# Two stacked cross-attention layers on one core: operands loaded already transposed, scalings broadcast through DRAM, the residual kept transposed

## The reference, cut to what matters

```
# layer 0, twice (s = "a" on ctx, s = "v" on fside), x: (128, 64, 128), ctx and fside: (128, 64, 64)
q = LN(x) @ Wq + bq;  k = LN(c) @ Wk + bk;  v = LN(c) @ Wv + bv          # LN with gain and bias, over the last axis
out_s = softmax(q k^T * 128**-0.5) v @ Wo + bo
r = out_a + out_v + x
x1 = LN(r) @ fc_W + fc_b + r
# layer 1, on ctx
w = softmax((x1 Wq1 + bq1)(ctx Wk1 + bk1)^T * 128**-0.5)
out = x1 + (w (ctx Wv1 + bv1)) @ Wo1 + bo1
```

## Time and profile before

| | us |
|---|---|
| device time, median of 3 runs | 169.53 (167.81 to 170.84) |
| span of the profiled execution, first to last instruction | 167.2 |
| its own device time | not listed apart from the three runs |
| PE busy, weight loads busy | 155.5, 121.7 |
| DVE, ACT, POOL busy | 131.4, 124.2, 76.4 |
| moved by DMA | 15.93 MB, of which 15.14 MB on SP's queue |

### The profile page before, as it was taken

How to read it: one execution, slowest core, us unless ns; L and a number is a source line. 1 busy time by engine, 2 the same in 40 slices (tenths; PEclk the granted TensorE clock), 3 DMA queues, 4 the chain that set the end, 5 groups by cost and what they waited for, 6 DMA issues and landing times.

```text
span 167.2 us, 6323 instructions
## 1 busy us (share of the span) xinstructions
PE 155.5 (93%) x2442; PEld 121.7 (73%) x2442; DVE 131.4 (79%) x400; ACT 124.2 (74%) x384; POOL 76.4 (46%) x104
## 2 busy tenths in 40 slices
PE   6799998999999999799999999989999999999682
PEld 6769674896689687767786787667788887995350
DVE  1693499999899789999999996497688997596531
ACT  3431559869988979599879788977978789866930
POOL 2026269789676523714979624194532022110210
PEclk9965579999999999999999999999999999999955
DMA  5999999900001010101010011001010100101113
GB/s 139 299 380 380 378 379 378 364 33 0 2 4 67 0 67 0 68 2 67 4 63 4 0 67 65 6 0 67 0 67 20 47 6 4 67 0 65 63 67 125
DMA packets 9982, 15.93 MB, mean 95 GB/s; under 512 B 1249, under 2 KB 3682, under 8 KB 9954
## 3 DMA queue, kind: packets, MB, share of 16 engines
q1 hardware_dynamic: 9522, 15.14, 25.1%
q10 hardware_dynamic: 432, 0.40, 1.0%
HBM read 11.35 MB, written 4.19 MB: 93 GB/s over the span
## 4 chain that ended last, share of the span: by engine, by line
PE 73%; DVE 9%; ACT 7%; issue 4%; DMA 3%; POOL 2%; ACTq 1%; POOLq 0%
PE ps L1526 9%; PE ps L1465 8%; PE ps L1508 7%; PE ps L1576 5%; PE ps L1516 5%; PE ps L1496 4%; PE ps L1541 4%; PE ps L1534 4%; PE ps L1485 4%; PE ps L1456 4%; PE ps L1475 4%; PE ps L1449 4%; DMA cf_sb<-in_cf 3%; PE ps L1568 3%; ACT exp L632 3%
## 5 line engine op out<-in xcount | busy, mean ns | idle before, releaser
L384 POOL TENSOR_TENSOR prob<-exp,rsum 128x512 f32<-128x512 f32 x16 | 16.7, 1042 | 23.5 <-DVE rsum L1025 23.5
L390 POOL TENSOR_TENSOR prob<-exp,rsum 128x256 f32<-128x256 f32 x16 | 9.8, 613 | 29.0 <-DVE rsum L1085 29.0
L356 POOL TENSOR_TENSOR z_sb<-x_sb,x_rstd 128x512 f32<-128x512 f32 x15 | 15.4, 1040 | 15.9 <-ACT x_rstd L543 14.1
L632 ACT ACTIVATE exp<-ps,exp_bias 128x64 f32<-128x64 f32 x64 | 19.2, 315 | 3.5 <-DVE exp_bias L1080 3.4
L1061 DVE SCALAR_TENSOR_TENSOR x_sb<-ps,res_rstd,res_sb 128x128 f32<-128x128 f32 x64 | 19.2, 342 | 0.2 <-issue 0.2
L1465 PE MATMUL ps<-zT_sb,m 128*128 128x512 f32 x32 | 17.8, 645 | 0.0
L1526 PE MATMUL ps<-wd,resT_sb 128*128 128x130 f32 x128 | 17.6, 280 | 0.0
L1508 PE MATMUL ps<-w,mix_sb 128*128 128x128 f32 x128 | 17.5, 280 | 0.0
L378 POOL TENSOR_TENSOR cfn_sb<-cf_scaled,cf_shift 128x512 f32<-128x512 f32 x15 | 15.6, 1042 | 4.0 <-issue 2.9
L1526 PEld LDWEIGHTS ps<-wd,resT_sb 128*128 128x128 f32 x128 | 15.6, 191 | 2.0 <-ACT resT_sb L609 1.5
L371 POOL TENSOR_TENSOR cf_scaled<-cf_sb,cf_rstd 128x512 f32<-128x512 f32 x15 | 15.4, 1043 | 2.7 <-ACT cf_rstd L555 2.5
(11 more groups left out here) (141 smaller groups left out, 384.2 us busy)
## 6 DMA issues: line engine op xcount, KB each, us to landing
x_sb<-in_x SPq DMA_DIRECT2D x16, 256.0 KB, 6.8
out<-out_sb SPq DMA_DIRECT2D x16, 256.0 KB, 2.0
cf_sb<-in_cf SPq DMA_DIRECT2D x15, 256.0 KB, 7.1
ct_sb<-in_ct SPq DMA_DIRECT2D x16, 128.0 KB, 7.9
w_sb<-in_w SPq DMA_DIRECT2D x1, 448.0 KB, 5.6
cf_sb<-in_cf ACTq DMA_DIRECT2D x1, 256.0 KB, 4.9
wq_sb<-in_wq ACTq DMA_DIRECT2D x1, 128.0 KB, 2.8
wt_sb<-in_wt SPq DMA_DIRECT2D x1, 128.0 KB, 4.0
```

Source lines behind the costliest of these rows:

```text
L356: pool.tensor_tensor(z_sb[:, g % Z_SLOTS, :, :], x_sb[:, g, :, :], wide_x(g), ALU.mult).then_inc(z_pool, 1)
L384: pool.tensor_tensor(prob0[:, g % PROB0_SLOTS, :, :, :], exp0[:, g % EXP0_SLOTS, :, :, :], wide0(rsum0, g), ALU.mult).then_inc(prob0_pool, 1)
L632: last = nc.scalar.activation(exp1[:, g % EXP1_SLOTS, p, :], ps[:, bank + u, v * S:(v + 1) * S], ACT.Exp, bias=exp1_bias[:, g, p:p + 1], a ...
```

## The change

What it does, in the order of a group's steps:

- The host gives two more arrays: `xt`, x transposed (256 KB a group), and `kt`, the keys transposed (256 KB a group). Inputs no longer stay whole in SBUF but go through rings (`X_SLOTS` 4, `XT_SLOTS` 8, `CF_SLOTS` 9, `KT_SLOTS` 3, `CT_SLOTS` 6), so loads on SP wait for readers.
- Groups 0 to 3 are normalized as before (`z`, `zT`, `scale_cf`, `shift_cf`, `cfT`). For groups 4 to 15 the normalizing is done on the transposed arrays. There the scalings lie along the free axis, the same for every partition. So for each of the batches 3 to 8 the scalings and shifts (`rows`, 40 columns) are transposed on PE (`turn_rows`), copied by ACT (`copy_rowsT`), stored to DRAM by SP (`store_rows`, 40 rows of 512 bytes), and read back by three SP transfers that fill all 128 partitions with 4 KB each: `spread_x` (every partition reads the same 4 KB), `spread_k` and `spread_s` (partitions 0 to 63 read one 4 KB piece, 64 to 127 another). As the transfers are issued, both sides of `spread_x` count 128 along their outermost dimension; `spread_k` and `spread_s` count 128 partitions on the SBUF side, but their DRAM side is 2 pieces, each repeated 64 times, so its outermost dimension counts 2. POOL then multiplies and adds whole tiles: `scale_xt`, `scale_kt`, `shift_kt`. `scale_cf` stays, for the values.
- `out0` is one product with 512 columns in place of four with 128, and comes out transposed. `residual` adds xt and a bias column and is kept transposed, so `copy_resT` goes; `resN` transposes it back for `stats_res`, which now reads PSUM.
- `x1` is split: ACT scales the four blocks of `dense` (`gain`), DVE makes the key biases (`key_biases`), PE transposes (`x1T`), DVE adds bias and residual in one instruction over 128 x 512 (`x1`); `copy_x1T` goes.
- For groups 1, 4, 7, 10, 13 and 15 `softmax0` takes its exponentials from PSUM in eight blocks of 64 columns, with the negated maximum as bias, and `diff_scores0` goes.
- Some folding work moves (biases of layer 0's output), more PE products without a use at the start (18 in place of 8), and all five orders are new.

The core of the diff:

```diff
+TURNED = [0, 1, 2, 3]
+BATCHES = [[0], [1], [2, 3], [4, 5], [6, 7], [8, 9], [10, 11], [12, 13], [14, 15]]
+SPREAD_FROM = 3
+EXP_BY_BLOCKS = [1, 4, 7, 10, 13, 15]
...
+            def store_rows(b):
+                at = b - SPREAD_FROM
+                sp.wait_ge(rowsT_copied, at + 1)
+                sp.dma_start(rows_dram[at, :, :], rowsT[:, at % SPREAD_SLOTS, :]).then_inc(rows_stored[at % SPREAD_SLOTS], 16)
+
+            def spread_x(b):
...
+                sp.dma_start(x_spread[:, at % SPREAD_SLOTS, :, :].rearrange("p g t -> p (g t)"),
+                             rows_dram[at, 0:8, :].rearrange("r t -> (r t)").unsqueeze(0).broadcast_to([D, 8 * P])
+                             ).then_inc(x_spread_in[at % SPREAD_SLOTS], 16)
+
+            def spread_k(b):
+                at = b - SPREAD_FROM
+                sp.wait_ge(rows_stored[at % SPREAD_SLOTS], 16 * (at // SPREAD_SLOTS + 1))
+                if at >= SPREAD_SLOTS:
+                    sp.wait_ge(ks_done, BATCHES[b - SPREAD_SLOTS][-1] + 1 - len(TURNED))
+                sp.dma_start(k_spread[:, at % SPREAD_SLOTS, :, :].rearrange("p g t -> p (g t)"),
+                             rows_dram[at, 8:24, :].rearrange("(h r) t -> h (r t)", h=2).unsqueeze(1
+                             ).broadcast_to([2, C, 8 * P])).then_inc(k_spread_in[at % SPREAD_SLOTS], 16)
...
+            def scale_kt(g):
...
+                spread_in(pool, k_spread_in, g)
+                need(pool, cfT_shifted, at - KS_SLOTS + 1)
+                pool.tensor_tensor(blocks(ks_sb[:, g % KS_SLOTS, :]), kt_sb[:, at % KT_SLOTS, :, :, :, :],
+                                   blocks(k_spread[:, slot, half, :]), ALU.mult).then_inc(ks_done, 1)
+
+            def shift_kt(g):
...
+                pool.wait_ge(ks_done, at + 1)
+                spread_in(pool, s_spread_in, g)
...
-            def softmax0(g):
-                act.wait_ge(diff0_done, g + 1)
-                prob0_ready(act, g - EXP0_SLOTS)
-                nc.scalar.activation(exp0[:, g % EXP0_SLOTS, :, :, :], diff0[:, g % DIFF0_SLOTS, :, :, :], ACT.Exp
-                                     ).then_inc(exp0_done, 1)
+            def softmax0(g, bank):
+                need(act, prob0_done, g - EXP0_SLOTS + 1)
+                if g in EXP_BY_BLOCKS:
+                    act.wait_ge(max0_done, g + 1)
+                    for h in range(2):
+                        for p in range(PAIRS):
+                            last = nc.scalar.activation(exp0[:, g % EXP0_SLOTS, h, p, :], ps[:, bank + h, p * S:(p + 1) * S],
+                                                        ACT.Exp, bias=max0[:, g % SLOTS, h, p:p + 1])
...
+            def gain(g, bank):
...
+                for p in range(PAIRS):
+                    at = (p % 2) * (D + 2)
+                    last = nc.scalar.mul(gain_sb[:, g % GAIN_SLOTS, p, :], ps[:, bank + p // 2, at:at + D],
+                                         res_rstd[:, g, p // 2, p % 2:p % 2 + 1])
...
+            def turn_rows(b, bank, *reads):
+                pe.wait_ge(x_rstd_done, b + 1)
+                pe.wait_ge(cf_shift_done, b + 1)
+                after(*reads)
+                nc.tensor.transpose(ps[0:40, bank, 0:P], rows[:, b, :], ident[:, :]).then_inc(rowsT_made, 1)
...
-                for u in range(DUOS):
-                    for v in range(2):
-                        p = 2 * u + v
-                        last = mm(ps[:, bank, p * P:(p + 1) * P], mix0_sb[:, g % MIX0_SLOTS, u, v, :, :], w01[:, 0:D],
-                                  start=True, stop=True)
-                last.then_inc(out0_made, 1)
+                mm(ps[:, bank, :], w01[:, 0:D], mix0_sb[:, g % MIX0_SLOTS, :, :, :, :], start=True, stop=True
+                   ).then_inc(out0_made, 1)
```

More of the change, by code:

```diff
@@ L294, in _ @@
-            load_x(7)
-            load_cf(7)
+            load_x(9)
+            store_rows(4)
+            load_kt(6)
+            load_x(10)
+            spread_s(4)
+            spread_x(4)
+            spread_k(4)
+            load_x(11)
+            load_kt(7)
+            load_xt(7)
+            load_xt(8)
+            load_x(12)
+            load_cf(9)
+            load_xt(9)
+            load_kt(8)
+            load_ct(4)
+            load_x(13)
+            load_xt(10)
+            load_cf(10)
@@ L305, in _ @@
+            store_rows(6)
+            spread_x(6)
+            spread_k(6)
+            store(1)
+            load_cf(12)
+            spread_s(6)
+            load_cf(13)
+            load_kt(11)
+            store(2)
+            load_kt(12)
+            load_xt(14)
+            load_kt(13)
+            load_x(15)
             load_ct(8)
-            load_x(11)
-            load_cf(11)
+            store_rows(7)
+            store(3)
+            spread_x(7)
+            load_cf(14)
             load_ct(9)
-            load_x(12)
@@ L837, in _ @@
[L837 to L852 removed]
+            copy_prob1T(7, 0)
+            copy_rowsT(8, 1)
@@ new lines, in _ @@
+            turn_rows(5, 5)
+            resN(4, 1)
+            s0(7, 2)
+            out1(0, 4, (rowsT_copied, 3))
+            out1(1, 0, (res_stats_done, 5))
+            t1(3, 7, (exp1_done, 3))
+            prob0T(5, 6)
+            prob1T(2, 5, (final_done, 1))
+            dense(4, 0, (final_done, 2))
+            mix1(2, 2)
+            s1(3, 4)
+            mix0(5, 6)
+            prob0T(6, 2, (mix1_copied, 3))
+            x1T(4, 3)
+            out0(5, 7)
+            prob0T(7, 6)
+            t1(4, 5, (exp1_done, 4))
@@ new lines, in _ @@
+            mix1(6, 4, (final_done, 5))
+            mix0(9, 2, (t1_copied, 8))
+            s1(7, 6, (mix1_copied, 6))
+            out1(5, 4, (mix1_copied, 7))
+            out0(9, 2)
+            prob0T(10, 0, (diff0_done, 8))
+            t0(12, 1)
+            dense(8, 3, (final_done, 6))
+            resN(9, 0, (prob0T_copied, 11))
+            mix0(10, 6, (exp1_done, 8))
+            t0(13, 2)
+            dense(9, 6, (mix0_copied, 11))
+            prob1T(7, 0, (res_stats_done, 10))
+            turn_rows(8, 1, (t0_copied, 13))
@@ new lines, in _ @@
+            x1T(8, 5)
+            s0(12, 3, (bias_row_done, 9))
+            out0(10, 0, (prob1T_copied, 8))
+            prob0T(11, 1, (rowsT_copied, 6))
+            t1(8, 2, (t0_copied, 14))
+            s0(13, 3, (diff0_done, 9))
+            mix1(7, 5, (bias_row_done, 10))
+            mix0(11, 0, (res_done, 11))
+            x1T(9, 7)
+            resN(10, 2, (t1_copied, 9))
+            dense(10, 5)
+            t1(9, 7)
+            out1(6, 3, (exp0_done, 14))
+            s1(8, 0, (mix0_copied, 12))
@@ L1870 @@
              np.pad(np.stack([take(n) for n in COLS64], axis=1), ((0, P - C), (0, 0)))], axis=1)),
-        "rows": np.ascontiguousarray(np.stack([take(n) for n in ROWS])[None]),
     }
```

1876 lines of the change are left out of this document (971 added, 905 removed).

## The result

The changed kernel takes 268.09 us (median of 4 runs, 266.93 to 269.42) against 169.70 for the kernel before in the same session: a ratio of 1.585 with a 95% interval of 1.573 to 1.597. It is slower, inside the predicted range of 205 to 273 and 18 us above the predicted 250. The profiled execution took 266.93 us, its span is 265.1.

The account below looks back on a forecast made before the run. PE bounded the kernel before; two DMA engines carrying the spreads would after. 24 + 132 + 8 + 35 + 15 = 214 us to the last spread, then `shift_kt` and 33: span 248, time 250, range 205 to 273.

Parts of the forecast that it names:

- The likeliest case: DMA: `k_spread` and `s_spread` run on two engines, 11.0 us each, 12 in series 132 us; chance 0.82.
- the idle time of the two engines: DMA: the two engines idle while the next scalings come, 5 times about 3 us, 15 us.
- the 35 us of other transfers: SP's queue: 51 transfers of 256 KB between the first store and the last `spread_s`, 0.69 us each, 35 us.
- The 205: Lower end of the predicted range: the time if a spread and its neighbour overlap in part.
- The end: After the last `spread_s`: `shift_kt` (1.04 us), `s0` of group 14 and 61 more PE steps, 33 us (30 to 41).
- PE's 10.4 us less: PE: `zT` and `cfT` go for 12 groups, `turn_rows` come, `out0` shortens; 10.4 us less, lost in PE's waits.
- where 6 was foreseen: ACT: copies of 34.6 us go, `gain` adds 17.3, exponential blocks add 11.3; net 6 us less.
- where 12.5 was charged: POOL: one more pass over 128 x 512 in 12 groups, at 1.04 us each, 12.5 us.
- the 1 us that I added for more POOL work: DVE's 32 small additions, slowed by POOL: 7 us already paid, a sixth more POOL work adds about 1.
- All 16 engines and in time: Rival, spreads: all 16 engines carry every spread and PE's savings show; span 155, time 158 us; chance 0.11.
- 16 engines, but the road is late: Rival, `turn_rows` to POOL: takes 16 us, late beyond 8.3; batches 3 to 5 each 8 late; 178 us; chance 0.03.
- Signs: Profile after: spreads 11 us or more, late loads, DMA share 0.1 to 0.3, POOL idle 80 us, PE clock partly low.

Follow-up runs that it names:

- by_group: `halves` with each spread issued apart for a batch's two groups (2048-byte packets, own semaphores): 167.4 us in four runs, 165.4 in six more, ratio 0.977.
- by_group_5: `by_group` without further edit, run again in the session of `rings`: 165.4 us, ratio 0.977 to the kernel before.
- rings: `by_group` with 10 ring slots for cf in place of 9 and 7 for xt in place of 8: 165.1 us, ratio 0.981.
- halves: Changed kernel with `k_spread` and `s_spread` each issued as two 64-partition transfers whose DRAM side counts 64 outermost: 174.2 us, ratio 1.029 to the kernel before.
- no_road: `halves` without the spreads of batches 5 to 8; POOL reuses the data of batches 3 and 4 (wrong scalings): 161.2 us, ratio 0.950.
- apart: `halves` with every partition reading its own 4 KB of x in all three spreads (wrong data): 169.8 us, ratio 0.996.
- next: `halves` with `k_spread` and `s_spread` directly behind `spread_x` in SP's queue: 172.4 us, ratio 1.015.

## Why the prediction was right, and where its sizes were off

**The mechanism.** The likeliest case, two engines for `k_spread` and `s_spread` in series with a sixteenth of everything else, is what happened: the count of closing packets, the two products one spread apart, and the runs with 2, 4 and 16 engines show it. The two packets of `rows_sb`, a single row, pointed to it beforehand. The Trainium skill's rule named above (the largest number up to 16 that divides both counts) and the reading by the smaller side lead to the same number here, 2; the ten closing packets of the store of 40 rows tell the two apart.

**The sum, term by term.** A spread takes 10.4 us by its packets (64 x 162 ns) where 11.0 was taken, 7 us less over twelve. The first store was issued at 20.84 and had landed by 22.17, against 24. The last spread landed at 224.0, not 214. The term that was too small is, for the most part, the idle time of the two engines, 5 times 3 us. From 24.2, when the last spread of batch 3 is issued, most of the time goes to spreads, but from the end of each batch's spreads to the next spreads there is more than the 3 us: `s_spread` of batch 3 lets POOL go on at 50.29, and the next spread is issued at 59.12, 8.8 us later. In between stand `scale_cf` and the two steps of `shifts` on POOL (L542, L532, L535), which are behind `shift_kt` in its queue, then 4 us until PE reaches `turn_rows`, with other groups' steps at a lowered clock ahead of it, and the store. For all five gaps and the 35 us of other transfers I had 50 us; the trace leaves (224.0 - 22.6) - 12 x 10.4 - 8 = 69. The packet records don't name the engine, so the 19 us can't be split for certain. But between the packets of one batch's spreads and the first of the next there are 11.3, 16.0, 4.3, 8.5 and 5.5 us, 46 in all, where I had 3 each. Some of the 35 us of other transfers lies in these gaps, some between the spreads.

**The range.** Its upper end adds up: 250 + 7 + 8 + 8 = 273. Its lower one does not: 7 us for the spreads, 2 for an earlier start, 5 for less idle time and 3 for a shorter end lead from 250 to 233, not to 225. The 205 rests on an overlap that no term prices. The measured 268 lies inside either way.

**The end.** From the last spread to the end it took 265.1 - 224.0 = 41 us, the upper bound, where I took 33 + 1. `shift_kt` of group 15 stands in POOL's queue behind seven other operations and began only at 233.49, and PE had 34.7 us of work after 225 us (last row under Signs), against the 29.3 of the steps that I counted. So 248 became 265 by -1.4 for the start, -7.2 for the spreads, +18.6 between them and +7 at the end: the terms partly cancel.

**The other engines.** PE's 10.4 us less show once the spreads are wide: 143.4 us in `by_group`, 12.1 less, though a part of that may be the granted clock, 0.977 there against 0.936 before. DVE has 7.6 us less, in the range of 7 to 12; `x1` takes 0.746, not 0.68. ACT has 5.8 less, where 6 was foreseen. POOL has 22.5 more where 12.5 was charged. 8 us of that is one price: a whole-tile operation with two full operands takes 1.27 us, not the 1.04 with a broadcast one, for all 36 of them. In the changed kernel:

```profile
L575 POOL TENSOR_TENSOR cfT_sb<-ks_sb,s_spread 128x512 f32<-128x512 f32 x12 | 15.2, 1266 | 49.1 <-issue 48.9
L542 POOL TENSOR_TENSOR cfv_sb<-cf_sb,rows 128x512 f32<-128x512 f32 x15 | 15.9, 1060 | 1.8 <-PE ps L1720 1.8
L836 ACT ACTIVATE gain_sb<-ps,res_rstd 128x128 f32<-128x128 f32 x64 | 18.3, 372 | 13.4 <-PE ps L1747 13.2
L809 ACT ACTIVATE exp<-ps,max 128x64 f32<-128x64 f32 x48 | 10.5, 341 | 0.0
L1270 DVE SCALAR_TENSOR_TENSOR x1T_sb<-ps,row_bias,resT_sb 128x512 f32<-128x512 f32 x16 | 11.9, 746 | 14.9 <-PE ps L1755 14.7
```

One product of `gain` takes 0.372 us, above the 0.27 that I had called its most. But 64 x 0.372 would be 23.8, and the row has 18.3 us busy: the products overlap, and each adds 0.29 to ACT's busy time. So `gain` costs 1.0 more than the 17.3 charged, and the 48 blocks, 0.341 each but 10.5 busy, cost 4.6 less than the 15.1 charged. The six copies of `rowsT`, 1.5 us, were not charged. With these terms put right the sum is 8 us less, not 6; 2 us of the measured 5.8 are not accounted for, and that the sum came out is luck in part. None of these prices touched the end, since every one of these engines waited for the spreads.

**POOL against DVE.** The small additions are two a group. The first of the kernel before is in the earlier trace rows; here the second, then the two of `by_group`:

```profile
L1080 DVE TENSOR_TENSOR exp_bias<-minus_top,bias_row 128x4 f32<-128x4 f32 x16 | 4.2, 262 | 0.5
```

```profile
L1295 DVE TENSOR_TENSOR exp_bias<-minus_top,bias_row 128x4 f32<-128x4 f32 x16 | 7.4, 462 | 0.4
L1290 DVE TENSOR_TENSOR minus_top<-minus_max,bias_row 128x4 f32<-128x4 f32 x16 | 3.8, 238 | 0.3
```

Before, both together took 5.7 + 4.2 = 9.9 us, of which 5.1 are above 32 x 0.15; my 7 had taken the first one's mean for both. In `by_group` they take 11.2, and 12.7 and 12.5 in `by_group_5` and `rings`. So the 1 us that I added for more POOL work did show, as 1 to 3, and the 33 that the Trainium skill's page "SBUF — State Buffer" would give at worst did not. Its word "fully blocks" fits single cases: in `halves` the shortest of the second additions takes 0.11 us, the median 0.164, and the longest 1.186, a whole POOL operation of 1.04 more.

**The rivals.** They were weighed wrongly against each other. "All 16 engines and in time", 158 us, had 0.11, and "16 engines, but the road is late", 178, had 0.03. The run with 16 engines took 174.2, and the road took 15.1 us from store to `shift_kt`, close to the 16 that this rival was worked out with. The point from which it decides, 8.3 us, was in the text, and so were the landings of 6.8 us that put the road beyond it; I should have given the late road the larger part. 158 us, or nearly, is what `no_road` shows (161.2) when the road of four of six batches is away.

**Signs.** The loads behind the spreads and POOL's idle time of 95.8 us are as named. The DMA share was to be one to three tenths all through and is somewhat higher, and the clock is low in parts. Stretches of the changed kernel:

```profile
20.00:50.00 30.00, 13.92 (x193) 10.28 (x191) 12.61 (x36) 11.60 (x37) 7.47 (x7) 0.84 0.39 122
150.00:200.00 50.00, 22.41 (x288) 14.23 (x289) 19.50 (x51) 17.16 (x64) 18.31 (x21) 0.67 0.34 115
225.00:265.00 40.00, 34.69 (x582) 23.50 (x582) 25.76 (x70) 28.96 (x123) 12.96 (x16) 0.96 0.15 56
```

## What to carry to other kernels

Before a transfer is priced by its bytes, count the outermost dimension on both sides: here 2, 4 and 64 repeats of the same bytes gave 276, 224 and 174 us, and the closing packets in the queue's row tell the number of engines without another run. A DMA share of a third can hide two engines that are full. A result that goes through DRAM and back is a loop, and must be laid out by its time from end to end (here 12 to 17 us). Loads that feed its next turn are better not pushed behind its own transfers: the order that did so took 171.6 us in place of 167.4.

## What the runs showed of the hardware that I had not expected

- A packet of 4096 bytes takes 162 ns in the median when two engines carry the spreads and 231 (253 in the mean) when 16 do, whether they read one address or many (`apart`); in `next` and `no_road` it is 266 and 268. All packets of 2048 bytes have a median of 84 ns in every run. The reason for the longer ones is open.
- GpSimd's `tensor_tensor` over 128 x 512 takes 1.27 us with two full operands and 1.04 to 1.06, in every row of 15 or 16 of them, with one broadcast along its innermost dimension. Of the three `shift_cf` in the changed kernel, also with one broadcast, two took 1.06 and one 1.58; why was not sought.
- The transfers of 40 rows ran on 10 engines, those of one row on one.
- Behind the two-engine spreads the issuing engine itself stood in the issue: 11.42 us for two transfers on SP, against 0.3 to 1.0 for one before them.
- ScalarE's product of 128 x 128 from PSUM with a scale for each partition takes 0.372 us from start to end, but in a row they overlap: 64 of them keep the engine busy for 18.3 us, 0.29 each.
